# Graph layer pair: counting the node-number rows inside the dst-ordered loop, in two PSUM banks freed by sharing

## The reference, cut to what matters

```
msg_1 = x @ W_m1.T + b_m1;  msg_2 = x @ W_m2.T + b_m2
msg_e = edge_attr @ W_me.T + b_me
msg   = relu(msg_1[src] + msg_2[dst] + msg_e)
msg   = relu(msg @ W_net.T + b_net)
agg   = segment_max(msg, src)          # 0 where a node has no edge
out   = x @ W_o1.T + b_o1 + agg @ W_o2.T + b_o2
```

## Time and profile before

| what | value |
|---|---|
| time, median of 3 runs (lowest to highest) | 4024.08 us (4019.18 to 4028.37) |
| profiled execution, its own time | 4000.34 us |
| its span, first to last instruction | 3998.6 us |
| mean granted TensorE clock | 0.846 of full speed |
| busy: TensorE, VectorE, ScalarE, GpSimd | 3124.2, 2115.7, 1055.7, 1922.2 us |

### The profile page before, as it was taken

How to read it: one execution, slowest core, us unless ns; L and a number is a source line. 1 busy time by engine, 2 the same in 40 slices (tenths; PEclk the granted TensorE clock), 3 DMA queues, 4 the chain that set the end, 5 groups by cost and what they waited for, 6 DMA issues and landing times. The chain is left out here.

```text
span 3998.6 us, 91262 instructions
## 1 busy us (share of the span) xinstructions
PE 3124.2 (78%) x22735; PEld 2371.3 (59%) x22736; DVE 2115.7 (53%) x9831; ACT 1055.7 (26%) x2227; POOL 1922.2 (48%) x2586
## 2 busy tenths in 40 slices
PE   6678777787787778886888884668887888888786
PEld 5455555555555555554666663546666766666676
DVE  7766656656666566654666663523333333333336
ACT  7023232322232323222333331211111111111112
POOL 1044555555455555554444345156666666666660
PEclk9778888888788888788999997878888888888888
DMA  4111111111111111115777776111111111111132
GB/s 149 28 28 31 31 31 31 31 30 31 29 30 30 29 30 30 30 21 130 179 181 177 178 180 162 31 41 42 43 42 43 42 41 43 43 41 43 43 41 40
DMA packets 583654, 245.36 MB, mean 61 GB/s; under 512 B 506959, under 2 KB 554394, under 8 KB 583336
## 3 DMA queue, kind: packets, MB, share of 16 engines
q1 hardware_dynamic: 528128, 142.56, 17.1%
q0 software_dynamic: 54816, 95.47, 9.4%
q10 hardware_dynamic: 648, 6.58, 0.5%
HBM read 151.83 MB, written 101.41 MB: 63 GB/s over the span
## 5 line engine op out<-in xcount | busy, mean ns | idle before, releaser
L933 POOL DMA_INDIRECT edge_in_src_order<-u,place x832 | 813.6, 978 | 806.8 <-DVE place L1015 415.5
L1459 POOL DMA_INDIRECT a_rows<-src_table,idx x832 | 792.3, 952 | 599.6 <-issue 281.7
L1522 PE MATMUL ps_s<-ohd_f,h 128*128 128x128 f32 x1664 | 406.2, 327 | 94.0 <-issue 91.7
L1154 POOL COPY m_s<-m 128x144 f32 x832 | 251.5, 345 | 348.5 <-PE ps_pre L1201 325.3
L992 DVE CUSTOM_DVE_ANT_0 junk<-ps_cnt,ohlo_a 128x128 bf16<-128x128 f32 x832 | 191.2, 284 | 421.5 <-PE ps_cnt L1042 218.3
L1489 DVE TENSOR_TENSOR ohd_f<-dloc_s,iota_f 128x512 f32<-128x512 f32 x208 | 144.0, 693 | 505.0 <-remote 444.5
L1513 PEld LDWEIGHTS ps_h<-bpart,dstT_b 128*128 128x128 f32 x1664 | 272.6, 236 | 208.3 <-issue 207.4
L1541 ACT ACTIVATE h<-ps_h 128x512 f32<-128x512 f32 x208 | 124.2, 597 | 1014.5 <-remote 661.2
L1523 PEld LDWEIGHTS ps_n<-onesf,ohd_f 128*128 128x128 f32 x1664 | 286.5, 212 | 106.5 <-issue 106.3
L1522 PEld LDWEIGHTS ps_s<-ohd_f,h 128*128 128x128 f32 x1664 | 286.2, 211 | 93.7 <-issue 90.8
L1476 DVE TENSOR_TENSOR hsumT<-hsumT,ps_s 128x128 f32 x832 | 239.7, 288 | 185.5 <-issue 80.2
(11 more groups left out here) (264 smaller groups left out, 5817.1 us busy)
## 6 DMA issues: line engine op xcount, KB each, us to landing
u_in<-edge_in_src_order SPq DMA_DIRECT2D x208, 192.0 KB, 3.9
running_max<-row SPq DMA_DIRECT2D x208, 192.0 KB, 2.9
rowt<-src_row SPq DMA_DIRECT2D x208, 130.0 KB, 3.8
key_in<-edge_keys SPq DMA_DIRECT2D x832, 2.0 KB
attr_in<-edge_attributes SPq DMA_DIRECT2D x832, 8.0 KB
edge_in_src_order<-u,place POOLq DMA_INDIRECT x832
a_rows<-src_table,idx POOLq DMA_INDIRECT x832
edge_attributes<-in_edge_attr ACTq DMA_DIRECT2D x8, 784.0 KB, 14.8
```

What stands on the lines that cost most here:

```text
L933: pool.indirect_dma_start(u_d, bass.IndirectOffsetOnAxis(place[:, u, j:j + 1], 0), ur[:, u, j, :], None, bounds_check=POS - 1, oob_is_err= ...
L1154: last = nc.gpsimd.tensor_copy(m1_s[:, u, j, :], m1[:].bitcast(F32)[:, bass.ds(at[j], 3 * F // 2)])
L1459: pool.indirect_dma_start(a_rows[:, u, j, :], None, a_d, bass.IndirectOffsetOnAxis(idx[:, u, j:j + 1], 0)).then_inc(got[u], 16)
L1522: m.matmul(ps_s[k][:, j, :], h[:, u, j, :], ohd[:, u, j, :], start=True, stop=True)
```

## The change

The counting of marks leaves the first stage and runs inside the dst-ordered loop. Every fourth slot VectorE makes the one-hot tables of one block (`ends`) and TensorE adds them into two banks `ps_ends` (`mark`); 52 such blocks, the last three with ends of -1, which match nothing. The scans, the small products, the shifts and the store of the rows follow the loop. Two banks are freed for this: `ps_eq` is one bank instead of two, and TensorE's list is put in another order, with `equal` after `count`; the transposed attributes go to the unused 128 columns of the bank of `ps_u` (`ps_attr`). Since TensorE and ScalarE then work in one bank, `turn` also waits until ScalarE has copied `ps_u` of an earlier group, and `product` until it has copied the attributes just transposed.

```
 first stage: the loop over NB on VectorE and TensorE, the scans, the shifts and the store of the rows are gone;
 left are at_f (ends of -1 behind the last block) and
+    v.tensor_scalar(firsts_c[0:hi - lo, q, :], ps_a[0:hi - lo, 4 * q:4 * q + 4], -float(P), float(P), ALU.mult, ALU.add)

 dst-ordered loop, VectorE
+    def ends(i, u, n):
+        if u == 0:
+            wait(dve, marked, n)
+            v.tensor_scalar(oh_group[:], iota_w[:, 0:G], at_f[:, 0, bass.ds(n, 1)], None, ALU.is_equal)
+            v.tensor_scalar(oh_slot[:], iota_w[:], at_f[:, 1, bass.ds(n, 1)], None, ALU.is_equal).then_inc(ends_ready, 1)
     pipeline(dve, G, [(0, local), (3, advance), (3, same_step), (0, invalid), (3, coarse),
-                      (4, across_steps), (3, fine), (0, keys), (4, put), (0, onehot)])
+                      (4, across_steps), (3, fine), (0, keys), (4, put), (0, onehot), (0, ends)])
+    dve.wait_ge(marked, G // 4 + 1)
     ...
 dst-ordered loop, TensorE
     def turn(i, u, n):
         ...
+        wait(pe, u_ready, i - 2)
-        m.transpose(ps_rec[:, 0:P], ...).then_inc(rec_turned, 1)
+        m.transpose(ps_attr, ...).then_inc(rec_turned, 1)
     def product(i, u, n):
-        pe.wait_ge(recT_ready, i + 1)
+        pe.wait_ge(recT_ready, i + 3 if not isinstance(i, int) else min(i + 3, G))
+    def mark(i, u, n):
+        if u == 0:
+            pe.wait_ge(ends_ready, n + 1)
+            first = isinstance(n, int) and n == 0
+            for q, (lo, hi) in enumerate(halves):
+                mm = m.matmul(ps_ends[q][0:hi - lo, :], oh_group[:, lo:hi], oh_slot[:], start=first, stop=False,
+                              skip_group_check=True)
+            mm.then_inc(marked, 1)
-    pipeline(pe, G, [(2, equal), (1, turn), (3, product), (3, count)])
+    pipeline(pe, G, [(1, turn), (3, product), (3, count), (2, equal), (1, mark)])
+    # once more the last (empty) block to close the sums, then the three small products, after the scans

 SyncE, after its loads
+    sp.wait_ge(rows_set, 8)
+    ... two stores of locs, and the wait for them
```

More of the change, by code:

```diff
@@ L191, in gnn @@
         pads_set = sem(whole, "pads_set")
+        above = sb(whole, "above", [P, P])
+        iota_w = sb(whole, "iota_w", [P, 512], F16)
+        one_w = sb(whole, "one_w", [P, 512])
+        at_f = sb(whole, "at_f", [P, 2, HB])
+        firsts_c = sb(whole, "firsts_c", [P, 2, 4])
+        halves = [(0, P), (P, G)]
         layer0 = ExitStack()
@@ L553, in _ @@
                             v.tensor_scalar(sf_row[:, h * HN:(h + 1) * HN], ps_x[0:1, 0:HN], 1.5 * F, -1.5 * F, ALU.mult, ALU.add).then_inc(to_pe, 1)
[L556 to L564, removed]
-                        for q, (lo, hi) in enumerate(halves):
[L566 to L576, removed]
+                        dve.wait_ge(to_dve, 11)
+                        for q, (lo, hi) in enumerate(halves):
+                            v.tensor_scalar(firsts_c[0:hi - lo, q, :], ps_a[0:hi - lo, 4 * q:4 * q + 4], -float(P), float(P), ALU.mult, ALU.add)
                     @block.tensor
@@ L879, in gnn @@
                 ur = sb(t, "u", [P, 4, 4, F])
-                ps_eq = [ps(t, f"ps_eq{k}", [P, 4, P]) for k in range(2)]
+                oh_group = sb(t, "oh_group", [P, G], F16)
+                oh_slot = sb(t, "oh_slot", [P, 512], F16)
+                passed_c = sb(t, "passed_c", [P, 2, 512])
+                base_c = sb(t, "base_c", [P, 2])
+                shift = sb(t, "shift", [P, 2, 4])
+                locs = sb(t, "locs", [P, 2, 512], BF16)
+                ps_eq = ps(t, "ps_eq", [P, 4, P])
+                ps_ends = [ps(t, f"ps_ends{k}", [P, 512]) for k in range(2)]
                 ps_cnt = [ps(t, f"ps_cnt{k}", [P, 4, P]) for k in range(2)]
-                ps_rec = ps(t, "ps_rec", [P, 512])
                 ps_oh = ps(t, "ps_oh", [P, 2, 512], F16)
@@ L905, in gnn @@
                 ones_set = sem(t, "ones_set")
+                ends_ready = sem(t, "ends_ready")
+                marked = sem(t, "marked")
+                ends_chain = sem(t, "ends_chain")
+                scanned = sem(t, "scanned")
+                based = sem(t, "based")
+                rows_set = sem(t, "rows_set")
+                row_stored = sem(t, "row_stored")
                 passed = sem(t, "passed_a")
@@ L984, in same_step @@
                             wait(dve, cnt_ready, i - 1)
-                            v.tensor_tensor(prior[:, u % 2], ps_eq[u % 2][:], bcast(earlier[:].unsqueeze(1), P, 4, P),
+                            v.tensor_tensor(prior[:, u % 2], ps_eq[:], bcast(earlier[:].unsqueeze(1), P, 4, P),
                                             ALU.mult).then_inc(prior_ready, 1)
@@ L1089, in turned @@
                             wait(act, sum_ready, i - 3)
-                            s.copy(attrT[:, u, :], ps_rec[:, 0:P]).then_inc(recT_ready, 1)
+                            s.copy(attrT[:, u, :], ps_attr).then_inc(recT_ready, 1)
                             act.wait_ge(new_ready, i + 1)
```

80 lines of the change are left out of this document (40 added, 40 removed).

## The result

The changed kernel took 4106.6 us (median of 4 runs, 4100.3 to 4110.8) where the kernel before took 4021.6 beside it: ratio 1.0205, 95% interval 1.0189 to 1.0221. That is 85 us more. The prediction had 195 more: the direction was right, the size more than twice too large, and 4107 lies near neither the forecast nor one of the rivals with a price of its own (4066, the nearest, was for another cause). The profiled execution after took 4104.2 us (span 4102.5).

What follows compares the result with a forecast made beforehand. The dst-ordered loop was taken as paced by signals between engines, held during GpSimd's send bursts. 4000.3 - 1 (stage and loop ends) + 196 (loop) = 4195, plus 23.7 to the median: 4219 us; range 4015 to 4350 (own range 4130 to 4360).

Steps and rivals of the forecast that it cites:

- End of the first stage: First stage loses its marking work but SyncE's pad stores are late next: 9.1 us shorter, not VectorE's 33.
- Marking in the loop: 52 blocks of one-hots and products in the loop, hidden: 0 us; at most 43 on TensorE, 36 on VectorE.
- Equal behind count: In the loop, prior then stands between release and next send: 0.87 us more, long intervals 8.93 us.
- The handshake: Two new TensorE waits over ps_u's shared bank: free outside a hold; held inside one, 37.4 us per four groups (+6.5).
- Sum for four groups: Loop's price per turn of four groups: +3.78 us, midway between two lower ways, over 52 turns 196 us.
- the second way: Short interval stays and the handshake passes early in the burst of eight: 33.7 us per turn, +2.8, loop +144.
- End of the loop: Scans, small products and rows after the loop, their signal held by the last sends: plus 8 us, 0 if it passes.
- the hold rule: In the loop, signals from about 1.3 us into a GpSimd send burst wait until about 1 us after its end.
- rival 1: Equal's old place was the price; the loop gains 55.8 us: 3967; chance 0.16 together with rival 4.
- rival 2: Nothing moves: the loop's hold ends with GpSimd's burst whatever TensorE did before: 4023; chance 0.09.
- rival 3: Only the added marking work shows in the loop, holds as today: +43 us, 4066; chance 0.13.
- rival 4: First stage gives back VectorE's whole 33 us, loop unaffected: 3991; chance 0.16 together with rival 1.

Runs made afterwards that it cites:

- e4: Changed kernel without marks in the loop, attributes in their own bank, equal back in two banks at its old place; 4014.1 us, ratio 0.9981.
- e1: Changed kernel without the 52 marking blocks in the loop, everything else of the change kept; 4112.9 us, ratio 1.0230.
- e5: Changed kernel with VectorE's reading of the counts and place moved ahead of prior; 3978.2 us, ratio 0.9975 to the kernel before.
- e2: Changed kernel without marks, transposed attributes in a bank of their own, equal still behind count; 4070.1 us, ratio 1.0124.
- e11: Kernel before with a GpSimd pause (memset of 2048 elements) between each group's second and third send; 3836.1 us, ratio 0.9526.
- e13: Changed kernel, prior still first, with a GpSimd pause (memset of 2048 elements) between second and third send; 3815.6 us, ratio 0.9565.
- e16: Changed kernel with counts read ahead of prior and a 16-element memset on GpSimd between second and third send; 3976.0 us, ratio 0.9971.
- e12: Changed kernel with counts read ahead of prior and a 2048-element memset on GpSimd between second and third send; 3833.1 us, ratio 0.9512.

## Why the prediction was right in direction and wrong in size

- **End of the first stage**: -9.1 forecast, -9.4 measured (first send 220.69, then 211.28). SyncE's pad stores were late next, as said, and e4, the first stage's gain with the loop of the kernel before, is 6 us faster.
- **Marking in the loop**: 0 forecast, 0 measured (e1). The Trainium skill ("SBUF — State Buffer", section "SBUF: two separate sides") says that VectorE in a two-port mode locks GpSimd out while it writes descriptors. The up to 36 us that the prediction worked out by it don't show in the time: without the one-hots of the marks it was 4112.9 against 4106.6. A small difference shows in the sends, which the prediction's reading of one turn missed: of the sends that ran beside one-hots of VectorE 83 of 342 took over 1.04 us in the changed kernel and 16 of 334 before, of the others 3 of 490 and 2 of 498. GpSimd, busy 830 us instead of 814, isn't the bound. Only one of the 90 sends beside the new one-hots was among the long ones, and no run shows whether VectorE was in such a mode.
- **Equal behind count**: right for the slots that wait for a release: 8.93 forecast, 8.92 measured (the median of the 55 intervals with a late signal), with prior's 0.88 us on the chain, and e5 shows it by taking prior off. But in 96 other intervals equal itself came late, median 9.34, a kind that the prediction didn't price, and 40 of the 57 intervals between 9.0 and 9.5 are of that kind: that so many lie near 8.93 is partly luck.
- **The handshake**: right in kind. The pair with the burst of eight was given 15.8 us where the handshake passes and 19.5 where it is held; it is 1012.65 - 996.48 = 16.2. It costs little alone (9 us) and 43 (e1 less e2) where equal stands behind count and the handshake pushes both into the burst. TensorE did product and count inside that burst, late, where the prediction had it stand still.
- **Sum for four groups: the step that failed.** I took +3.78 us per turn, 196 in all, midway between "the short interval is gone" and "it stays and the handshake passes". Measured is 95.7 / 52 = 1.84 per turn. The short interval did not go, so the second way's +2.8 (144 us) was the one to take: 52 us of the miss are that choice. Most of the other 48 lies in the intervals outside the pairs. A pair (an interval under 6 us and the next one) went from 14.4 us on average to 15.6, +1.2, as the second way had it (15.83 against 14.59). The 106 intervals outside pairs should have gained 0.76 each (8.93 against the mean of 8.28 and 8.06); their median did, from 8.11 to 9.01, but their mean went only from 8.12 to 8.47, since 30 of them still lay between 6 and 8 us, 15 of these under 7 where before there were 6. That is 0.41 x 106 = 43 us less. I had priced every such interval as held for the full time and multiplied one pattern by 52 turns; the loop drifts between patterns, and in the 30 intervals VectorE read the counts 2.5 to 5.3 us after the first send, where the prediction had 6.7.
- **End of the loop**: +8 forecast, +0.5 measured. The rows of VectorE at the loop's end:

```profile
1891.82 2.32 DVE L1007 TENSOR_TENSOR_SCAN passed_c<-one_w,ps_ends 128x512 f32<-128x512 f32 x2
1895.36 0.16 DVE L1012 COPY base_c<-ps_eq 128x1 f32<-128x1 f32 x1 [1.21 <-PE ps_eq L1096]
```

The last burst began at 1890.20. Two signals, VectorE to TensorE and back, passed 4 and 5 us into it, where the hold rule would have kept them until the end. So that rule, as the prediction put it, is not general.

- **Rivals**: rival 1 (equal's old place was the price) is refuted by e2 against e4, 56 us slower with the new place; rival 2 (nothing moves) by the 85 us; rival 3's marks cost nothing (e1); rival 4 (33 us from the first stage) is refuted by the 9.4 us.

## What to carry to other kernels

When a chain of engines is paced by releases after a burst, first look at what stands between the release and the next burst: moving two entries in one engine's list (e5) was worth as much as undoing the change. Before one pattern's price is multiplied by the number of turns, count over the whole loop how often each pattern occurs. Look at the granted clock stretch by stretch: here it fell to 0.50 behind a burst of eight, and the next slot took 8.7 us instead of 5.7. And where an engine's back-to-back DMA issue slows others, try a gap in it: a pause of an engine that wasn't the bound bought nearly 5% here.

## What the hardware showed that I had not expected

The prediction spoke of signals that are held. The rows show that while GpSimd sends back to back, instructions that wait for nothing are late as well: the counting products above, 0.5 to 1.2 us apart, and in the kernel before VectorE's one-hots, which wait for no signal once they have begun:

```profile
1025.94 0.23 DVE L977 TENSOR_SCALAR ohhi_a<-iota_b,him 128x64 f16<-128x64 bf16 x1
1026.95 0.44 DVE L977 TENSOR_SCALAR ohhi_a<-iota_b,him 128x64 f16<-128x64 bf16 x1 [0.79 <-issue]
1027.65 0.25 DVE L977 TENSOR_SCALAR ohhi_a<-iota_b,him 128x64 f16<-128x64 bf16 x1 [0.26 <-issue]
1028.37 0.30 DVE L977 TENSOR_SCALAR ohhi_a<-iota_b,him 128x64 f16<-128x64 bf16 x1 [0.46 <-issue]
```

So what the bursts slow seems to be the issue of instructions on the other engines rather than signals; the few instructions of the loop's end, which ran through the last burst unhindered, would fit if they had been issued before it. That is argued from rows, not shown: no run here separates the two, nor tells why the sends do it. Shown is that breaking the row of sends decides, with all sends made (e11 to e13), that the slowing ends with time without sends and not with another instruction between them (e16 against e12), and that a pause of 0.52 us is too short, 0.95 enough for part of the groups, and 1.27 for most.
